# Products of zeros on TensorE ahead of the first transposes and behind the first twenty steps of a chunked recurrence

## The reference

```python
h = take(W.T, x)                                  # 2048 rows of 128
xb = einsum('btd,hd->bth', layernorm(h), B)
s  = tanh(s @ A.T + xb_t)                         # over the 512 positions; states
g  = sigmoid((states @ C.T) @ Wg.T + bg) * (states @ C.T)
h  = h + g @ Wo.T + bo
xf = layernorm(h)
h  = h + top-1 of 8 experts: (silu(xf @ w1.T) * (xf @ w3.T)) @ w2.T
       + gelu(xf @ sw1.T) @ sw2.T
```

## Time and profile before

| | us |
|---|---|
| median of 3 executions | 182.56 (180.62 to 183.18) |
| the profiled execution | 182.58 |
| its span, first to last instruction | 180.7 |
| TensorE busy | 138.5 |
| VectorE busy | 127.2 |
| ScalarE busy | 104.7 |
| GpSimd busy | 84.1 |
| mean granted clock of TensorE | 0.971 |

### The profile page before, as it was taken

How to read it: one execution, slowest core, us unless ns; L and a number is a source line. 1 busy time by engine, 2 the same in 40 slices (tenths; PEclk the granted TensorE clock), 3 DMA queues, 4 the chain that set the end, 5 groups by cost and what they waited for, 6 DMA issues and landing times.

```text
span 180.7 us, 3231 instructions
## 1 busy us (share of the span) xinstructions
PE 138.5 (77%) x997; PEld 99.7 (55%) x997; DVE 127.2 (70%) x365; ACT 104.7 (58%) x239; POOL 84.1 (47%) x77
## 2 busy tenths in 40 slices
PE   0105997788898888886799988899939989999720
PEld 0104864666675666675445878466726657666510
DVE  1245676927499995999779899488825778887730
ACT  2001444589989983587779993675532645655400
POOL 3768874900000000343100658552687787886580
PEclk9999999969999999999999999999996999999995
DMA  4564345899000000012200033410122443433331
GB/s 153 150 184 138 97 140 195 278 384 365 7 0 0 4 0 4 2 60 95 79 4 0 29 91 114 134 32 16 47 45 31 45 42 33 44 33 34 29 33 15
DMA packets 9955, 14.37 MB, mean 80 GB/s; under 512 B 1936, under 2 KB 4624, under 8 KB 9936
## 3 DMA queue, kind: packets, MB, share of 16 engines
q1 hardware_dynamic: 5904, 10.45, 16.9%
q0 software_dynamic: 4032, 3.67, 13.3%
HBM read 10.71 MB, written 3.41 MB: 78 GB/s over the span
## 4 chain that ended last, share of the span: by engine, by line
DMA 22%; PE 20%; POOL 18%; DVE 14%; ACT 12%; issue 10%; POOLq 1%; SPq 1%; DVEq 0%
DMA w_sb<-x_rows,row_in 7%; PE bank L655 6%; POOL w_sb L415 6%; POOL emb_rows L371 5%; DMA emb_rows<-emb,tok_sb 5%; POOL out L422 4%; PE bank L680 4%; DMA xblk<-x_rows,row_in 4%; ACT attn_out L725 4%; DMA w_sb<-w 3%; ACT states L702 3%; ACT w_hl L742 3%; PE bank L478 2%; PE bank L668 2%; DMA out<-w_sb,row_of 2%
## 5 line engine op out<-in xcount | busy, mean ns | idle before, releaser
L422 POOL DMA_INDIRECT out<-w_sb,row_of x20 | 31.3, 1564 | 9.1 <-DVE w_sb L1205 4.8
L478 PE MATMUL bank<-states,sq_sb 128*128 128x128 f32 x108 | 27.1, 335 | 6.0 <-ACT states L702 1.6
L655 PE MATMUL bank<-w_hl,xblk_t 128*128 x120 | 30.4, 391 | 1.0 <-issue 1.0
L403 POOL TENSOR_TENSOR rstd<-vareps,cst 128x2 f32<-128x2 f32 x8 | 5.7, 710 | 45.7 <-DVE vareps L853 45.7
L478 PEld LDWEIGHTS bank<-states,sq_sb 128*128 128x128 f32 x108 | 17.4, 202 | 14.2 <-ACT states L702 13.8
L812 ACT ACTIVATE w_sb<-bank,factor 128x512 f32<-128x512 f32 x20 | 13.8, 688 | 19.4 <-PE bank L655 19.3
L476 PE MATMUL bank<-x_in,sq_sb 128*128 128x128 f32 x108 | 23.3, 299 | 1.6 <-ACT x_in L695 1.5
L415 POOL DMA_INDIRECT w_sb<-x_rows,row_in x16 | 17.5, 1094 | 12.4 <-issue 6.3
L702 ACT ACTIVATE states<-bank 128x128 f32<-128x128 f32 x54 | 14.9, 276 | 12.2 <-PE bank L478 12.0
L680 PE MATMUL bank<-w_hl,w_sb 128*128 x160 | 16.6, 246 | 5.7 <-DVE w_sb L1205 5.7
L476 PEld LDWEIGHTS bank<-x_in,sq_sb 128*128 128x128 f32 x108 | 17.9, 207 | 2.8 <-ACT x_in L695 1.6
(11 more groups left out here) (160 smaller groups left out, 288.9 us busy)
## 6 DMA issues: line engine op xcount, KB each, us to landing
w_sb<-w SPq DMA_DIRECT2D x24, 256.0 KB, 6.4
x_rows<-norm SPq DMA_DIRECT2D x4, 256.0 KB, 2.4
out<-attn_out SPq DMA_DIRECT2D x4, 256.0 KB, 3.1
late<-places SPq DMA_DIRECT2D x1, 619.5 KB, 8.3
sw_sb<-sw SPq DMA_DIRECT2D x2, 256.0 KB, 3.0
cst<-consts SPq DMA_DIRECT2D x1, 420.0 KB, 3.3
sq_sb<-sq SPq DMA_DIRECT2D x1, 384.0 KB, 3.7
out<-w_sb,row_of POOLq DMA_INDIRECT x20, 3.3
```

What stands on the lines that cost most here:

```text
L422: pool.indirect_dma_start(out=out, out_offset=bass.IndirectOffsetOnAxis(ap=row_of[:, k:k + 1], axis=0), in_=out_blk[k % RING], in_offset=N ...
L478: pe.matmul(pre, at, states[:, i * COLS:(i + 1) * COLS], start=False, stop=True).then_inc(pre_ready, 1)
L655: mm = pe.matmul(hb[:], xblk_t[:, k % 3, b * P:(b + 1) * P], w[:, bass.ds(e * INNER + a * EXPERTS * INNER, INNER)], start=(j == 0), stop=( ...
```

## The change

VectorE's clearing of `zeros` now raises a semaphore. TensorE waits for it after its first product (L456), then runs 28 products of the zero tile with its own first column repeated 512 times, all into bank 6, ahead of the transposes of pair 0. One more stands behind those transposes. Behind the two products of each of steps 0 to 19, and ahead of any transposes that follow that step, stand further ones: one each, and two each for steps 8 to 13. That makes 28 + 1 + 26 = 55, and nobody reads what they write.

```diff
+HUM_BEFORE = 28
+HUM = {i: 2 if 8 <= i < 14 else 1 for i in range(20)}
...
+            def hum(count):
+                for _ in range(count):
+                    pe.matmul(bank[6][:], zeros[:], zeros[:, 0:1].to_broadcast([P, GC]), start=True, stop=True)
+
+            pe.wait_ge(zeros_set, 1)
+            hum(HUM_BEFORE)
             turn_pair(0)
             pe.wait_ge(pads_zero, 1)
+            hum(1)
...
             for i in range(STEPS - 1):
                 advance(i)
+                hum(HUM.get(i, 0))
                 if i in TURN_AT:
                     turn_pair(TURN_AT[i])
...
-            dve.memset(zeros[:], 0.0)
+            dve.memset(zeros[:], 0.0).then_inc(zeros_set, 1)
```

More of the change, by code:

```diff
@@ L269, in build @@
         late_in = sem("late_in")
+        zeros_set = sem("zeros_set")
         gathered = [sem(f"gathered{n}") for n in range(PAIRS)]
```

## The result

| | before | after |
|---|---|---|
| median of 5 executions | 181.78 us (180.62 to 183.18) | 186.96 us (186.38 to 188.72) |
| ratio | | 1.034, interval 1.029 to 1.039 |
| the profiled execution, its span | 182.58, 180.7 | 188.72, 186.9 |
| TensorE busy, products and weight loads | 138.5 us, 997 each | 148.6 us, 1052 each |

A forecast was written before the change was run, and what follows sets the result against it. The prediction took the recurrence to be the bound, held by gathers and weights until 36.12 us, then by the engines. Zero terms and -0.88 took the span from 180.7 to 179.8, plus 1.88 outside: 181.7 us, range 180.2 to 183.7.

The forecast's parts named there:

- What one product of zeros costs: On TensorE, one 512-column product of zeros occupies 0.22 us at full clock, 0.41 us at half, at most 0.38 without overlap.
- So the gathers behind it stay where they are. Term: 0: Row gathers behind VectorE's third normalise at 16.71 us: the 28 early products don't delay them; term 0 (to +0.3).
- 0.93 us of cover: Waits of the squares of steps 16 and 17 for weights (0.36 and 0.57 us), set against a 0.6 us delay.
- The 28 ahead of pair 0: TensorE's free 7.74 us before the first transposes: 28 products need 6.2 us at full clock, 11.5 at half; term 0.
- Steps 9 to 13: Two products behind a step: pair 6 turned at 28.6 us, step 14 0.6 us late but covered by weight waits; term 0.
- Steps 14 to 19: term -0.88: Recurrence around 37 us: one product per step keeps the clock full, removing the half-clock dip and 0.88 us.
- the dip stays: Rival for the dip at 37 us: the clock still falls or the gain is swallowed, 182.6 us; chance 0.22.
- It fills the stretch: 31.57 to 37.05 us: added products bring 2.1 us to TensorE's 3.78 of 5.48 us busy, over the 85% that kept the clock.
- The slow rival: Products of zeros don't raise TensorE's clock, the 28 all run at half clock, total 195 us; chance 0.06.
- 181.7 + 1.2: Forecast time plus the delay past the cover in steps 9 to 13 if a product takes 0.38 us.
- the rival without overlap: Products of zeros take 0.38 us each, the 28 end 2.9 us late, total 183.5 us; chance 0.08 with like delays.

The follow-up runs named there:

- tiny_55: The change with its 55 products of zeros at 1 column in place of 512; ratio to before 1.036 (1.026 to 1.045).
- zeros_and_90_tiny: The change plus 90 more products of one column ahead of the 28; ratio to before 1.005 (1.002 to 1.009), median 183.73 us.
- zeros_no_branch: The change with TensorE running the version for 20 blocks straight on, without its branch after the 18th block; ratio to before 1.000 (0.992 to 1.007).
- before_no_branch: The kernel before the change, with TensorE's branch after the 18th block taken out; ratio to before 0.997 (0.992 to 1.002).
- tiny_30: The kernel before with 30 products of one column ahead of pair 0; four executions, 183.12 to 191.45 us, no ratio.
- tiny_145: The change plus 90 products of one column ahead, its own 55 products also at 1 column; ratio to before 1.011 (1.003 to 1.019).
- late_10: The kernel before with only ten products of zeros, one behind each of steps 10 to 19; ratio to before 1.005 (1.000 to 1.009).
- ahead_10: The change with 10 products of zeros ahead of pair 0 in place of 28; ratio to before 1.010 (1.006 to 1.013).
- twins: The change plus 90 one-column products ahead, its 55 products at 512 columns against 1; ratios to before 1.004 (0.999 to 1.008) and 1.011 (1.003 to 1.019).

## Why the prediction was wrong

- *The step that failed is the sum's silent one.* The forecast costs a product of zeros by its place on the array alone ("What one product of zeros costs", 0.22 us). It left out that each is two instructions to be brought in, and so put the length of the program at nothing without a reason. That made 3.0 us of pause, and 1.55 behind it with the clock at half for a part, at a branch 150 us later, which no term and no rival names. tiny_55 shows it without the array's work, zeros_and_90_tiny and zeros_no_branch take it away with the work kept.
- *"So the gathers behind it stay where they are. Term: 0"* failed too. VectorE's third normalise did stay (16.78 against 16.71), as argued; but the last gather became 1.9 us longer, beside a packet that before came 10 us later (that the packet is the cause is not shown). The 0.93 us of cover did not help: the weights are held until the gather is in and landed 1.0 later themselves, so step 18 was still 1.85 late after 2.03 at step 14, and only the dip that was gone brought step 22 to 0.97.
- *The 28 ahead of pair 0* were right: they took 7.54 us, from 7.03 to 14.57, between the 6.2 of full clock and the 11.5 of half, and nothing waited for them.
- *Steps 9 to 13* were right for TensorE: 0.22 us each, pair 6 at 28.83 against 28.6. Pair 7 then waited for the late rows and not for the zeros.
- *Steps 14 to 19: term -0.88.* The forecast came out in this one trace (3.42 against 4.30, clock 1.00), but neither its size nor its mechanism is shown. The size: the dip stands in the one trace of before, but not in before_no_branch, tiny_30 or tiny_145, which have none of the zeros' work either and no late gather, so in one trace of four; late_10 has no dip and no gain. The mechanism: with zeros behind steps 0 to 19 the dip is absent in five traces (ahead_10 among them) and there in the sixth, zeros_no_branch (the rival "the dip stays" in that trace). "It fills the stretch" is the step that doesn't hold there: a product of zeros comes only with its step, and the steps of that stretch wait for weights. And the share of busy time that I set against it (69% lost, 85% kept) was no criterion: before_no_branch kept the clock at 60%.
- *The slow rival* (zeros don't raise the clock) was wrong: the 28 did not all run at half clock (7.54 us, not 11.5), the first transposes took 0.59 in place of 0.73, and the second pair's 0.38 in place of 0.63. In the six traces with ten or more zero products of 512 columns ahead of pair 0, the clock's first recorded change, to 1.0, is at 9.6 to 12.4 us, in the eight others at 20.0 to 23.7. What the Trainium skill says, that the gate acts on how busy the engine has been (TensorE: Matmul & The Clock Gate, "What's actually happening"), agrees with this for the rise; the fall in zeros_no_branch and its absence in before_no_branch are not told apart by it. The remark of the Trainium skill on the peak-current limit, that operands of all zeros don't trip it (the same page, "Seeing it yourself"), does not carry over to this gate. That the total was slower was not this rival's doing.
- *The range.* Its upper end was not where the sum puts it: 181.7 + 1.2 is 182.9, and 183.5 is the rival without overlap. Either lies below the 186.96 measured.

## What to carry to other kernels

An instruction costs its place in the program too. Before adding filler to an engine that has a branch or a jump ahead, count the instructions, look in the trace at where the packets of instructions fall and at the "issue" idle behind each jump, and compare with the same number of instructions that do nothing. Where a kernel becomes slower by a change that cannot cost that much, take the work out of the added instructions and leave them in: one run tells code from work. And filler that stands behind the real work in an engine's queue stops when that work waits (1.93 us idle in zeros_no_branch, with the dip behind it); it is no cover for the waits of others.

## What the runs showed of the hardware

- Behind a jump over the version for 23 blocks (113 products, so at least 226 instructions) TensorE went on at once (0.23 to 0.30 us) up to a fixed place in its program, and there waited until 2.5 to 3.3 us after the start of the next 16 KB packet. With 30 added products the pause was 0.94 us, with 55 it was 3.3 to 3.6, and with 145 it was as before (0.23 and 0.30).
- The last gather of 128 rows took 3.81 to 5.08 us in the six traces where a 16 KB packet of instructions started beside it, and 2.97 to 3.37 in the eight others. It is not shown that the packet is the cause.
- Products of a zero tile raise the granted clock: its first recorded change, to 1.0, came at 9.6 to 12.4 us with them and at 20.0 to 23.7 without. They did not keep it up in every trace: in zeros_no_branch it was at half from 39.25 to 42.66, after TensorE had stood idle for 1.93 us.
- A clock dip in one trace need not be in the others: of four traces without the zeros' work and without a late gather, one had it.

**Left open.** Whether the zeros' work is a gain by itself (twins 0.7% apart, intervals overlapping) and whether it keeps the clock up; what makes the last gather late; why zeros_and_90_tiny and late_10 are 0.5% above before; and what made the 0.7 us between step 22 and the branch, of which 0.5 lie behind the first product of the blocks. No version that was run is faster than before beyond its interval.
